# Second expert layer: the last gathers and adds by pieces of 128 tokens instead of by batches of 100

## The reference, cut to what matters

```python
x = x + _L1_ffn_ref(_layernorm(x), gate_w, w1, w2, sw1, sw2)

shared = silu(xf @ sw1[0]) @ sw2[0]             # xf: 1600 tokens x 256
scores = sigmoid(xf @ gate_w.T)                 # 16 experts in 4 groups
...                                             # best 2 groups, then the best 2 experts in them
tw = tw / (tw.sum(axis=-1, keepdims=True) + 1e-20)
combine = zeros.at[arange(N)[:, None], ti].add(tw)
out = shared
for e in range(16):
    out = out + combine[:, e:e+1] * (silu(xf @ w1[e]) @ w2[e])
```

## Time and profile before

| | us |
|---|---|
| median of three runs | 1813.96 |
| the profiled execution's own time | 1814.75 |
| its span | 1813.0 |
| TensorE busy | 1618.7 (89%) |
| VectorE busy | 1229.8 (68%) |
| ScalarE busy | 741.9 (41%) |
| GpSimd busy | 920.7 (51%) |

### The profile page before, as it was taken

One profiled execution on the slowest core, in us unless ns is written; L12 is line 12 of the kernel. 1 busy time (PEld: TensorE's weight loads), 2 busy tenths in 40 slices (PEclk: granted clock), 3 DMA queues, 4 the chain that ended last, 5 costly groups with the idle time before them and its releaser, 6 DMA issues. The chain is left out here.

```text
span 1813.0 us, 27644 instructions
## 1 busy us (share of the span) xinstructions
PE 1618.7 (89%) x8770; PEld 1109.1 (61%) x8770; DVE 1229.8 (68%) x2197; ACT 741.9 (41%) x1965; POOL 920.7 (51%) x799
## 2 busy tenths in 40 slices
PE   4999977999999999999999996699999389979980
PEld 3677753555555555555555554399999267665770
DVE  5598768777777777777777744566666757656433
ACT  2100102444454444444444442366666256652220
POOL 0378756777888777778887452123332000000536
PEclk9999986999999999999999997699999799988895
DMA  6434345122212212222212001664443520001433
GB/s 200 131 67 94 70 96 151 42 79 79 63 53 79 79 53 69 79 79 79 59 58 79 11 11 47 237 212 131 138 139 110 162 53 1 0 4 40 120 112 108
DMA packets 91472, 157.41 MB, mean 87 GB/s; under 512 B 45841, under 2 KB 70645, under 8 KB 88077
## 3 DMA queue, kind: packets, MB, share of 16 engines
q1 hardware_dynamic: 84301, 138.86, 26.2%
q0 software_dynamic: 7040, 16.92, 3.3%
HBM read 125.31 MB, written 28.48 MB: 85 GB/s over the span
## 5 line engine op out<-in xcount | busy, mean ns | idle before, releaser
L897 ACT ACTIVATE R<-banks 128x400 f32<-128x400 f32 x768 | 326.7, 510 | 318.4 <-PE banks L931 317.6
L713 DVE TENSOR_REDUCE PM<-banks 128x2 f32<-128x964 f32 x320 | 360.8, 1132 | 138.2 <-PE banks L690 138.1
L751 POOL TENSOR_TENSOR EA<-EA,R 128x400 f32<-128x400 f32 x288 | 306.4, 1064 | 119.7 <-ACT R L897 106.3
L931 PE MATMUL banks<-QS,KH 128*128 128x400 f32 x768 | 288.9, 376 | 2.4 <-DMA QB<-ML 2.4
L931 PE MATMUL banks<-QB,KB 128*128 128x400 f32 x768 | 265.8, 346 | 0.0
L731 DVE TENSOR_TENSOR banks<-banks,R 128x400 f32<-128x400 f32 x320 | 183.7, 574 | 27.9 <-ACT R L897 26.7
L540 POOL TENSOR_TENSOR arena<-arena 96x400 f32<-96x400 f32 x128 | 141.4, 1124 | 117.4 <-DVE arena L515 117.3
L941 PE MATMUL banks<-R,KV 128*64 128x400 f32 x960 | 187.5, 512 | 0.0
L931 PEld LDWEIGHTS banks<-QS,KH 128*128 128x128 f32 x768 | 145.1, 189 | 54.7 <-issue 37.9
L690 PE MATMUL banks<-KH,QS 64*128 64x482 f32 x320 | 160.9, 504 | 17.2 <-DVE PM L713 7.7
L690 PEld LDWEIGHTS banks<-KH,QS 64*128 64x128 f32 x320 | 60.9, 191 | 160.6 <-DVE PM L713 86.4
(11 more groups left out here) (288 smaller groups left out, 3227.6 us busy)
## 6 DMA issues: line engine op xcount, KB each, us to landing
arena<-in_ctx_T SPq DMA_DIRECT2D x16, 1444.0 KB
m_stage_d<-in_m_down SPq DMA_DIRECT2D x32, 672.0 KB
QS<-queries SPq DMA_DIRECT2D x16, 800.0 KB, 6.8
m_up<-in_m_up SPq DMA_DIRECT2D x8, 1392.0 KB, 12.3
queries<-q_out_h SPq DMA_DIRECT2D x64, 100.0 KB, 2.4
queries<-q_out_l SPq DMA_DIRECT2D x64, 100.0 KB, 2.4
QB<-queries SPq DMA_DIRECT2D x16, 400.0 KB, 8.0
arena<-recips SPq DMA_DIRECT2D x32, 200.0 KB
```

The source lines that it names most:

```text
L713: nc.vector.tensor_reduce(PM[:, 2 * i:2 * i + n], banks[:, k:k + n, 0:KW], AX.X, ALU.max).then_inc(red_done, 1)
L751: nc.gpsimd.tensor_tensor(out, first, tile_of(n, 1), ALU.add).then_inc(odd_sum, 1)
L897: nc.scalar.activation(tile_of(n, o), psum[ring_bank(score_tile(b, n, o))][:, 0:CH], ACT.Exp).then_inc(exp_done, 1)
L931: last = nc.tensor.matmul(out, lhs[r][:, keys], heads[:, o], start=lhs is KH, stop=lhs is KB)
```

## The change

The closing part no longer goes by batches but by pieces of 128 tokens, counted through all batches: 12 pieces of 128 and one of 64. For that the token rows, the two shares and the two slots of each token are needed with the partition as "token number modulo 128" instead of "place in the batch". A new class, `FlatTokens`, brings them there through three new DRAM tensors. The shares and slots are stored by four DMAs on ScalarE's queue before its first tile, and loaded by eight DMAs on the same queue after its work of step 20; in all of them the contiguous run on the DRAM side and the SBUF side is one 4-byte number. X is stored two batches at a time by SyncE behind the result stores of tiles 3 to 10, and loaded behind that of tile 14 into `f_X`. The buffer of the gathered rows becomes a ring of eight pieces.

```diff
+class FlatTokens:
+    PIECES, RING = -(-B * S // P), 8
+    FULL = B * S // P
+    REST = B * S - FULL * P
+    ...
+    def store_lists(self, d, nc):
+        for at, rows in ((self.dram["w"], d.w[:, 2:4, :]), (self.dram["slots"], d.slots[:].rearrange("s (n b) -> s n b", n=2))):
+            for n in range(2):
+                nc.scalar.dma_start(at[n].rearrange("(b s) -> s b", s=S), rows[:, n],
+                                    allow_slow_non_contiguous=True).then_inc(self.lists_out, 16)
+
+    def load_lists(self, act, nc):
+        act.wait_ge(self.lists_out, 64)
+        full = self.FULL * P
+        for at, rows in ((self.dram["w"], self.w), (self.dram["slots"], self.slots)):
+            for n in range(2):
+                nc.scalar.dma_start(rows[:, n, 0:self.FULL],
+                                    at[n, 0:full].rearrange("(j p) -> p j", p=P),
+                                    allow_slow_non_contiguous=True).then_inc(self.lists_in, 16)
+                nc.scalar.dma_start(rows[0:self.REST, n, self.FULL:], at[n, full:].rearrange("(p o) -> p o", o=1),
+                                    allow_slow_non_contiguous=True).then_inc(self.lists_in, 16)
+
+    def store_rows(self, sp, X, m):
+        rows = slice(2 * m, 2 * m + 2)
+        sp.dma_start(self.dram["x"].rearrange("(b s) d -> s b d", s=S)[:, rows], X[:, rows, :]).then_inc(self.rows_out, 16)
+
+    def load_rows(self, sp):
+        sp.wait_ge(self.rows_out, 16 * (B // 2))
+        full = self.FULL * P
+        sp.dma_start(self.X[:, 0:self.FULL, :], self.dram["x"][0:full].rearrange("(j p) d -> p j d", p=P)).then_inc(self.rows_in, 16)
+        sp.dma_start(self.X[0:self.REST, self.FULL, :], self.dram["x"][full:]).then_inc(self.rows_in, 16)
 ...
                 for k in range(tiles):                                    # SyncE
                     sp.wait_ge(y_done, k + 1)
                     sp.dma_start(results[k * TOK1:(k + 1) * TOK1], ys[:, k % YBUFS, :]).then_inc(stored[k % YBUFS], 16)
-                for b in range(B):
-                    sp.wait_ge(added, b + 1)
-                    sp.dma_start(out[b], X[:, b, :]).then_inc(written, 16)
+                    if ADD_AT <= k < ADD_AT + PAIRS:
+                        sp.wait_ge(s_added, k - ADD_AT + 1)
+                        flat.store_rows(sp, X, k - ADD_AT)
+                    if k == ADD_AT + PAIRS + 3:
+                        flat.load_rows(sp)
+                tokens = out.rearrange("b s d -> (b s) d")
+                for j in range(flat.PIECES):
+                    sp.wait_ge(added, j + 1)
+                    sp.dma_start(tokens[j * P:j * P + flat.height(j)], flat.X[0:flat.height(j), j, :]).then_inc(written, 16)
 ...
-                for b in range(B):                                        # GpSimd
+                pool.wait_ge(flat.lists_in, 16 * 8)
+                for j in range(flat.PIECES):
+                    if j >= flat.RING:
+                        pool.wait_ge(added, j - flat.RING + 1)
                     for n in range(2):
-                        pool.indirect_dma_start(back[:, b, n, :], None, results[0:tiles * TOK1, :],
-                                                bass.IndirectOffsetOnAxis(d.slots[:, n * B + b:n * B + b + 1], 0)).then_inc(back_in[b], 16)
+                        pool.indirect_dma_start(flat.back[0:flat.height(j), j % flat.RING, n, :], None, results[0:tiles * TOK1, :],
+                                                bass.IndirectOffsetOnAxis(flat.slots[0:flat.height(j), n, j:j + 1], 0)).then_inc(back_in[j], 16)
 ...
+                flat.store_lists(d, nc)                                   # ScalarE
                 for k in range(tiles + 1):
                     if k < tiles:
                         silu(k)
                     if k:
                         hidden_out(k - 1)
+                    if k == tiles // 2:
+                        flat.load_lists(act, nc)
 ...
-                v.wait_ge(s_added, PAIRS)                                 # VectorE
-                for b in range(B):
-                    v.wait_ge(back_in[b], 32)
+                v.wait_ge(flat.rows_in, 32)
+                v.wait_ge(flat.lists_in, 16 * 8)
+                for j in range(flat.PIECES):
+                    v.wait_ge(back_in[j], 32)
+                    rows = slice(0, flat.height(j))
                     for n in range(2):
-                        ins = nc.vector.scalar_tensor_tensor(X[:, b, :], back[:, b, n, :], d.w[:, 2 + n, b:b + 1],
-                                                             X[:, b, :], ALU.mult, ALU.add)
+                        ins = nc.vector.scalar_tensor_tensor(flat.X[rows, j, :], flat.back[rows, j % flat.RING, n, :], flat.w[rows, n, j:j + 1],
+                                                             flat.X[rows, j, :], ALU.mult, ALU.add)
```

More of the change, by code:

```diff
@@ L1811, in gather, with __init__, height @@
                                 bass.IndirectOffsetOnAxis(d.source[:, k:k + 1], 0)).then_inc(self.x_in[k % self.BUFS], 16)
-def grouped_moe(core, dram, X, ident, normed, results, weights, buffers, out):
+class FlatTokens:
+    PIECES, RING = -(-B * S // P), 8
+    FULL = B * S // P
+    REST = B * S - FULL * P
+    def __init__(self, core, ctx, dram):
+        nc = core.nc
+        self.dram = dram
+        self.X = fixed(ctx, nc, "f_X", [P, self.PIECES, D])
+        self.back = fixed(ctx, nc, "f_back", [P, self.RING, 2, D])
+        self.w = fixed(ctx, nc, "f_w", [P, 2, self.PIECES])
+        self.slots = fixed(ctx, nc, "f_slots", [P, 2, self.PIECES], U32)
+        self.lists_out = core.sem("f_listsout")
+        self.lists_in = core.sem("f_listsin")
+        self.rows_out = core.sem("f_rowsout")
+        self.rows_in = core.sem("f_rowsin")
+    def height(self, j):
+        return P if j < self.FULL else self.REST
+    def store_lists(self, d, nc):
[21 more added lines that the diff above has]
+        sp.dma_start(self.X[0:self.REST, self.FULL, :], self.dram["x"][full:]).then_inc(self.rows_in, 16)
@@ L1816, in grouped_moe @@
+def grouped_moe(core, dram, X, ident, normed, results, weights, buffers, flat_dram, out):
     nc, psum = core.nc, core.psum
@@ L1892, in _, with grouped_experts @@
                 d.vector(v)
-        grouped_experts(core, X, ident, d, shared, weights, rows, results, out)
-def grouped_experts(core, X, ident, d, shared, weights, rows, results, out):
+        grouped_experts(core, X, ident, d, shared, weights, rows, results, flat_dram, out)
+def grouped_experts(core, X, ident, d, shared, weights, rows, results, flat_dram, out):
     nc, psum = core.nc, core.psum
@@ L1909, in grouped_experts @@
         ys = fixed(ctx, nc, "g_ys", [P, YBUFS, D])
-        back = fixed(ctx, nc, "g_back", [S, B, 2, D])
+        flat = FlatTokens(core, ctx, flat_dram)
         s_added = core.sem("g_sadded")
@@ L1921, in grouped_experts @@
         stored = [core.sem(f"g_stored{u}") for u in range(YBUFS)]
-        back_in = [core.sem(f"g_back{b}") for b in range(B)]
+        back_in = [core.sem(f"g_back{j}") for j in range(flat.PIECES)]
         first_in = core.sem("g_firstin")
@@ L1933, in _ @@
                     sp.dma_start(results[k * TOK1:(k + 1) * TOK1], ys[:, k % YBUFS, :]).then_inc(stored[k % YBUFS], 16)
-                for b in range(B):
-                    sp.wait_ge(added, b + 1)
-                    sp.dma_start(out[b], X[:, b, :]).then_inc(written, 16)
-                sp.wait_ge(written, 16 * B)
+                    if ADD_AT <= k < ADD_AT + PAIRS:
[7 more added lines that the diff above has]
+                    sp.dma_start(tokens[j * P:j * P + flat.height(j)], flat.X[0:flat.height(j), j, :]).then_inc(written, 16)
+                sp.wait_ge(written, 16 * flat.PIECES)
             @block.gpsimd
@@ L2050, in _ @@
                         nc.vector.tensor_tensor(X[:, rows, :], X[:, rows, :], shared[:, rows, :], ALU.add).then_inc(s_added, 1)
-                v.wait_ge(s_added, PAIRS)
-                for b in range(B):
-                    v.wait_ge(back_in[b], 32)
+                v.wait_ge(flat.rows_in, 32)
[3 more added lines that the diff above has]
+                    rows = slice(0, flat.height(j))
                     for n in range(2):
-                        ins = nc.vector.scalar_tensor_tensor(X[:, b, :], back[:, b, n, :], d.w[:, 2 + n, b:b + 1],
-                                                             X[:, b, :], ALU.mult, ALU.add)
+                        ins = nc.vector.scalar_tensor_tensor(flat.X[rows, j, :], flat.back[rows, j % flat.RING, n, :], flat.w[rows, n, j:j + 1],
+                                                             flat.X[rows, j, :], ALU.mult, ALU.add)
                         ins.then_inc(added if n else first_in, 1)
                         if not n:
-                            v.wait_ge(first_in, b + 1)
+                            v.wait_ge(first_in, j + 1)
 class CausalLatents:
@@ L2420, in model @@
```

(4 more changed lines are left out.)

## The result

The changed kernel took 1832.24 us (median of four runs, 1831.59 to 1833.64), the kernel before 1813.93 on the same chip (four runs, 1813.88 to 1815.54): ratio 1.01, 95% interval 1.0082 to 1.0117. Forecast were 1819.2 and a range to 1832. The sign was right; the size, +18.3 instead of +5.2, was not, and the median lies 0.2 us outside the range. Between the two profiled executions the span grew by 16.8 us (1813.0 to 1829.8).

The account below looks back on a forecast made before the run. The prediction took GpSimd's gathers to bound the closing and TensorE the tiles before it. It summed -9.0 + 6.9 + 2.0 + 4.6 + 0.7 = +5.2 us, giving 1819.2 us, range 1805 to 1832.

Parts of the forecast that it names:

- The bound: GpSimd's row gathers alone bound the closing part; TensorE bounds the expert tiles before it, 1.90 us each.
- term 1: Closing part: 32 gathers become 26, 1.25 us apart, saving 9.0 us.
- Term 2: List stores on ScalarE's queue before the first tile: +6.9 us of stall and +2.0 us of colder TensorE clock.
- the price of one element: List stores before the first tile: 29 ns per 4-byte element, taken from 400-byte stores, between ends of 12 and 50.
- Term 2's count: List stores before the first tile: ScalarE comes free, at 1693.2, once 375 elements per engine have been executed.
- what of it lies on the path: Before the first tile: silu(0) waits behind the list stores on ScalarE and TensorE waits for it, +6.9 us.
- term 3: List loads on ScalarE in tile step 20: held 7.2 us, 2.6 covered, +4.6 us, plus 0.7 of clock.
- The clock: TensorE warms up again after idling: +2.0 us behind the list stores, +0.7 behind the list loads.
- term 4: X stored and loaded through DRAM on SyncE: load some 8 us, cost 0, at most +2 if result stores wait.
- B: List stores and loads: elements are dear at 50 ns, +23 us, total 1837; chance 0.15.
- C: Each list issue holds ScalarE until its own descriptors are out: stores +4.6 us more, total +9.9, 1824; chance 0.18.
- A: ScalarE before silu(0): list elements are cheap (12 ns) or taken at once; total 1807 or 1805; chance 0.25.

Follow-up runs that it names:

- e_none: The changed kernel with no lists through DRAM: slots counted on chip, shares all 0.5, X still through DRAM; 1804.67 us, ratio 0.9941.
- e_load: e_none plus eight list loads of the same patterns in step 20, from an input into unused tiles; 1812.21 us, ratio 0.9987.
- e_hold: The changed kernel with GpSimd's gathers of tiles 3 and on waiting until the list stores have landed; 1837.25 us, ratio 1.0123.
- e_pad_hold: The changed kernel with each list number on its own 512 bytes of DRAM, gathers of tiles 3 and on held until list stores land; 1825.37 us, ratio 1.0057.
- e_half: e_none plus only the two list stores of the shares, 3200 elements, never loaded; 1818.36 us, ratio 1.0022.
- e_turn: The changed kernel with lists transposed on TensorE, stored by SyncE as 400-byte runs, loaded as rows and turned back; 1806.33 us, ratio 0.9952.

## Why the prediction was right in sign and wrong in size

- **The bound and term 1** held. The period of the 128-row gather, taken from the other end of the same stage, was 1.253 us against 1.25, and the closing gained 9.6 us against 9.0. e_none shows 8.8 to 10.7, with an interval (6.9 to 14.5) that holds both.
- **Term 2 failed**, and with it the total. Its step "the price of one element" took 29 ns from 400-byte stores. Behind their burst packed numbers cost 42 ns alone and more beside gathers, padded ones 16. The stores cost 18.9 us where 8.9 were summed. The row of 400-byte stores couldn't have shown it: padded, the same stores cost, by ratios, 2.5 + 10.7 - 8.3 = 4.9 us, if the loads cost what they do in e_load.
- **Term 2's count** was too low as well. It had ScalarE free after 375 elements per engine. In e_hold and e_pad_hold 4237 and 4250 list packets had started by then, in the changed kernel 4738, on ten engines 424, 425 and 474. At the 29 ns of the forecast that is an estimated 1.4 to 2.9 us; the price of the element is the larger part.
- **Also in term 2**, the step "what of it lies on the path" was wrong in kind. It let the stores act through ScalarE alone, since ScalarE stands behind them in order. The gathers of tiles 3 and on were under way at the same time, and I priced the gathers' effect on the loads (term 3) but never the stores' effect on the gathers. e_half shows that this second way is enough by itself: 14.7 us with ScalarE not held.
- **The clock** term was right as a mechanism and on the low side: +2.0 and +0.7 were put down; both gaps show some four us of work at 1.2 GHz, 8 matmuls per two us instead of 14, so an estimated two us each, where the first work of the stage ran at 1.2 GHz in both kernels.
- **Term 3**: forecast 4.6 + 0.7, measured 8.3 by the ratios (7.5 by the medians). ScalarE was held 9.0 us against 7.2. The element was cheaper than thought (2269 packets in two us on 16 engines are 14 ns each, against 22), but X's load, which term 4 put at some 8 us, had been issued only 6 us before and was still moving; 2.3 us of the hold are its. The terms were summed side by side where one ran into the next.
- **Term 4**: 0 to +2 was put down; 1.1 us are seen in e_none, through the very wait that was named, and none in e_turn. Its load of X was not free all the same, since it lengthened the list loads.
- **The rivals.** B (50 ns, 1837) had the size of the elements about right but gave the loads 12.8 us; they are cheap. C, held until its own descriptors are out, failed with the room of 105 that it assumed: in e_half the second store's issue returns in 0.96 us with most of its elements still to go. With room for some 215 per engine it would fit the 424 above as well as the forecast's rule fits with some 56, and no run tells them apart. Neither explains the second load issue of the changed kernel, 64 numbers held 2.87 us while none of the 1600 numbers issued by then had started. A was wrong for the packed lists; its figure, 1805 to 1807, is what e_turn reached.
- **Left open**: where the first 2500 elements wait that are taken in fast and land late, where a gather's packet waits when it takes 2.9 us, and what holds an issuing engine. No run separated these.

## What to carry to other kernels

Ask of every new DMA not only how long it holds its issuer but which transfers under way it can slow, and count elements, not bytes: here 25 KB in single numbers cost more than 1.6 MB in rows. Don't write thousands of single neighbouring numbers to DRAM beside work that needs it; turn them on TensorE first, or, if they must go singly, give each 64 bytes, which took most of the loss away here. When a large gain meets an unexplained loss, take the two apart by leaving the added part out: e_none showed at once that the idea was sound and its transport was not.

## What the runs showed of the hardware

- Stores of packed 4-byte numbers start at over 1200 per us at first (1481 in some 1.2 us) and at 240 per us later, and 6400 of them land 26.7 us after the first issue (e_hold); with 512 bytes for each they land after 10.9 us (e_pad_hold).
- Such stores slow a different queue's gathers far beyond a fair share: 2.9 us per gather packet in 1684 to 1688, where 144 of them took 36.3% of 4 us before, 0.16 us each. The Trainium skill (DMA: Bandwidth & Descriptors, Queues, rings and completion order) has each engine alternate between its queues, 9 to 17 descriptors of one at a time. One turn of the lists would then hold many slow elements (at the 42 ns of e_hold an estimated 0.4 to 0.7 us), less than the 2.9 us seen; and in e_half gather packets still take an estimated 0.8 us while hardly a list packet starts, so by this trace alternating is not the whole of it.
- How long an issue holds its engine depends on what went before it: the first store of 1600 elements returned in 0.57 us, before any of them had started, and the third and fourth of the same size were held 13.6 and 9.6.
- The indirect gather of 128 rows repeats every 1.25 us, one of 100 rows every 1.30: between these two its period doesn't grow with its rows.
